# A new order of VectorE's work in the attention groups: key counts in two halves around the masks, zero ranks ahead of the queries

## What is computed

```python
h = _layernorm(x) * (1 + ca) + sa
q, k, v = (sparsify(proj(w), keep=1) for w in (wq, wk, wv))   # the largest |feature| of 16 is kept
scores = q @ k.T / sqrt(16), causal
keep the 64 largest scores of each row, softmax over them, times v, times wo
x = x + ga * attention
h = _layernorm(x) * (1 + cb) + sb
x = x + gb * experts(h)      # each expert takes its 512 best tokens of 4096
```

## Time and profile before

| | |
|---|---|
| median of 3 runs | 1072.18 us (1070.66 to 1073.46) |
| the profiled execution's own time | 1072.58 us |
| its span, first to last instruction | 1070.7 us |
| TensorE (PE) busy | 919.0 us, 86% |
| VectorE (DVE) busy | 662.1 us, 62% |
| ScalarE (ACT) busy | 480.0 us, 45% |
| GpSimd (POOL) busy | 270.0 us, 25% |
| mean granted TensorE clock | 0.912 |

### The profile page before, as it was taken

How to read it: one execution, slowest core, us unless ns; L and a number is a source line. 1 busy time by engine, 2 the same in 40 slices (tenths; PEclk the granted TensorE clock), 3 DMA queues, 4 the chain that set the end, 5 groups by cost and what they waited for, 6 DMA issues and landing times. The chain is left out here.

```text
span 1070.7 us, 17237 instructions
## 1 busy us (share of the span) xinstructions
PE 919.0 (86%) x6504; PEld 497.5 (46%) x6504; DVE 662.1 (62%) x1462; ACT 480.0 (45%) x631; POOL 270.0 (25%) x403
## 2 busy tenths in 40 slices
PE   6778999898999888999999999996213999999996
PEld 4533443334444453534335445335102666666664
DVE  6758667567677666686784784625486655543441
ACT  2635667764667746476665554661000122221110
POOL 3503212411322402132320210001003433334222
PEclk9779999999999989999988998897555999999999
DMA  4000000000100001100002012001651144442211
GB/s 149 10 1 21 1 21 1 2 1 2 60 21 1 1 27 56 60 1 2 2 1 81 2 41 81 1 1 40 219 197 41 46 114 105 113 114 40 25 20 20
DMA packets 34854, 46.57 MB, mean 43 GB/s; under 512 B 2184, under 2 KB 30928, under 8 KB 34640
## 3 DMA queue, kind: packets, MB, share of 16 engines
q1 hardware_dynamic: 28624, 36.89, 10.3%
q0 software_dynamic: 6144, 8.52, 4.9%
HBM read 32.69 MB, written 12.72 MB: 42 GB/s over the span
## 5 line engine op out<-in xcount | busy, mean ns | idle before, releaser
L947 ACT ACTIVATE p_buf<-ps 128x1024 f32<-128x1024 f32 x288 | 279.4, 1023 | 182.7 <-PE ps L424 98.7
L424 PE MATMUL ps<-qx,kd 32*128 32x512 f32 (+3 forms) x1280 | 149.0, 542 | 29.9 <-DVE p_buf L1281 26.1
L457 PE MATMUL ps<-p_buf,vv 128*17 128x512 f32 (+3 forms) x1664 | 160.2, 487 | 0.0
L2096 ACT ACTIVATE h_t<-ps,b_t 128x512 f32<-128x512 f32 x64 | 44.0, 687 | 239.7 <-PE ps L2036 239.7
L1281 DVE SCALAR_TENSOR_TENSOR p_buf<-ps,p_buf 128x1024 f32<-128x1024 f32 x64 | 76.7, 1220 | 76.6 <-ACT p_buf L947 63.5
L2036 PE MATMUL ps<-tok_t,w_sb 128*128 128x512 f32 x256 | 114.2, 605 | 0.5 <-DVEq L2143 0.5
L2046 PE MATMUL ps<-w_sb,h_t 128*128 128x256 f32 x512 | 112.5, 380 | 0.8 <-ACT h_t L2096 0.8
L779 POOL TENSOR_SCALAR_AFFINE_SELECT p_buf<-p_buf 128x512 f32<-128x512 f32 x64 | 42.0, 669 | 274.2 <-ACT p_buf L947 271.5
L2046 PEld LDWEIGHTS ps<-w_sb,h_t 128*128 128x128 f32 x512 | 96.6, 190 | 15.3 <-ACT h_t L2096 1.6
L424 PEld LDWEIGHTS ps<-qx,kd 32*128 32x128 f32 x1280 | 55.8, 193 | 72.5 <-issue 57.1
L365 PE MATMUL ps<-w_t,h_t 128*128 128x512 f32 (+1 forms) x224 | 78.8, 496 | 0.8 <-ACT w_t L889 0.8
(11 more groups left out here) (293 smaller groups left out, 1392.9 us busy)
## 6 DMA issues: line engine op xcount, KB each, us to landing
w_sb<-in_L_ffn_w_dram SPq DMA_DIRECT2D x16, 1024.0 KB, 8.5
h_table<-xr SPq DMA_DIRECT2D x3, 1056.0 KB, 4.6
x_in<-in_L_attn_x_dram SPq DMA_DIRECT2D x6, 512.0 KB, 3.9
out_dram<-xr SPq DMA_DIRECT2D x3, 1024.0 KB, 5.2
xr<-in_L_attn_x_dram SPq DMA_DIRECT2D x3, 1024.0 KB, 5.7
h_table<-xr SPq DMA_DIRECT2D x2, 528.0 KB, 3.1
xr<-in_L_attn_x_dram SPq DMA_DIRECT2D x2, 512.0 KB, 5.4
p_buf<-in_L_wmod_dram SPq DMA_DIRECT2D x1, 1024.0 KB, 8.6
```

The lines of the kernel that those rows point to most:

```text
L424: m = pe.matmul(o, key, qx[r, par, t0:t0 + w], start=True, stop=not early)
L457: m = pe.matmul(ps[32 * h:32 * h + HD + 1, 6, o:o + w], vv[:, (gi // NG) % 2, i, HG * (gi % NG) + h, :], p_of(gi, u)[:, h, lo:lo + w], sta ...
L947: act.activation(p_of(gi, u)[:, 2 * a:2 * a + 2, :], buf(w), ACT.Exp, scale=0.25).then_inc(free_of(w)[0], 1)
L2096: act.activation(h1_t[:, f, :], ps[:, L1_BANKS[f % 3], :], ACT.Relu, bias=b1_t[:, e * FO + f:e * FO + f + 1]).then_inc(s_h1, 1)
```

## The change

It touches VectorE's queue alone; no instruction of another engine moves. `key_counts` becomes `counts_first` (tokens 0 to 511, waits for K0 only) ahead of the second masks and `counts_second` (tokens 512 to 1023, waits for K1, starts from the copied last count) behind them. `keys` becomes `key_maxima`, `key_kinds` and `keys_shifted`; the turned outputs are written between them. `zero_rank` moves ahead of `queries`. The `one_feature` step of the second tile moves behind the second masks, that of the third behind the shifted keys, that of the fourth behind `losers`; `feature_limits` also goes behind `losers`. `normalize(b + 1, 0)` moves from ahead of the second masks to behind the turned outputs.

```diff
-                def key_counts(n):
-                    kx = kd[:, n % 2, :]
+                def counts_first(n):
+                    h = slice(0, 512)
+                    dve.wait_ge(f_mfree, m_at["K0", n] + 1)
+                    dve.tensor_scalar(k_not[:, h], kd[:, n % 2, h], 0.0, None, ALU.is_le)
+                    dve.drain()
+                    dve.tensor_tensor_scan(left[:, h], k_not[:, h], minus1[:, :].to_broadcast([P, 512]), TOPK + 0.5,
+                                           ALU.add, ALU.add)
+
+                def counts_second(n):
+                    h = slice(512, T)
                     dve.wait_ge(f_mfree, m_at["K1", n] + 1)
-                    dve.tensor_scalar(k_not[:, :], kx, 0.0, None, ALU.is_le)
-                    dve.drain()
-                    dve.tensor_tensor_scan(left[:, :], k_not[:, :], minus1[:, :].to_broadcast([P, T]), TOPK + 0.5,
+                    dve.drain()
+                    dve.tensor_copy(carry[:, :], left[:, 511:512])
+                    dve.tensor_scalar(k_not[:, h], kd[:, n % 2, h], 0.0, None, ALU.is_le)
+                    dve.drain()
+                    dve.tensor_tensor_scan(left[:, h], k_not[:, h], minus1[:, :].to_broadcast([P, 512]), carry[:, :],
                                            ALU.add, ALU.add)
                     dve.drain().then_inc(f_cnr, 1)
...
                     if more:
-                        key_counts(n)
-                    if g == 0 and pre:
-                        normalize(b + 1, 0)
+                        counts_first(n)
+                    mask(gi, 1, 0)
+                    mask(gi, 1, 1)
                     if tiles:
                         one_feature(b + 1, t0 + 1)
-                    mask(gi, 1, 0)
-                    mask(gi, 1, 1)
+                    if more:
+                        counts_second(n)
                     if post and g == norm_group(b - 1):
                         second_norm(b - 1, 1)
                     if g == 1 and pre:
                         norm_stats(b + 1, 1)
                     if more:
-                        keys(n)
-                    if tiles:
-                        one_feature(b + 1, t0 + 2)
+                        key_maxima(n)
+                    if more and not (post and g == norm_group(b - 1)):
+                        key_kinds(n)
                     out_rows_of(gi, 0)
+                    if g == 0 and pre:
+                        normalize(b + 1, 0)
+                    if more and post and g == norm_group(b - 1):
+                        key_kinds(n)
...
                     if more:
-                        queries(n)
+                        keys_shifted(n)
+                    if tiles:
+                        one_feature(b + 1, t0 + 2)
                     if g == 0 and post:
                         residual(b - 1, 0)
                     if more:
                         zero_rank(n)
+                    if more:
+                        queries(n)
                     if g == 1 and pre:
                         normalize(b + 1, 1)
                     if g == 0 and pre:
                         modulate(b + 1, 0)
+                    if more:
+                        losers(n)
                     if tiles:
                         one_feature(b + 1, t0 + 3)
                     if g == 3 and pre:
                         feature_limits(b + 1)
-                    if more:
-                        losers(n)
                     if g == 0 and post:
                         residual(b - 1, 1)
```

More of the change, by code:

```diff
@@ L1217, in feature_limits, with key_maxima @@
                     dve.drain()
-                def key_counts(n):
-                    kx = kd[:, n % 2, :]
+                def counts_first(n):
[7 more added lines that the diff above has]
+                    h = slice(512, T)
                     dve.wait_ge(f_mfree, m_at["K1", n] + 1)
-                    dve.tensor_scalar(k_not[:, :], kx, 0.0, None, ALU.is_le)
                     dve.drain()
-                    dve.tensor_tensor_scan(left[:, :], k_not[:, :], minus1[:, :].to_broadcast([P, T]), TOPK + 0.5,
+                    dve.tensor_copy(carry[:, :], left[:, 511:512])
+                    dve.tensor_scalar(k_not[:, h], kd[:, n % 2, h], 0.0, None, ALU.is_le)
+                    dve.drain()
+                    dve.tensor_tensor_scan(left[:, h], k_not[:, h], minus1[:, :].to_broadcast([P, 512]), carry[:, :],
                                            ALU.add, ALU.add)
                     dve.drain().then_inc(f_cnr, 1)
-                def keys(n):
-                    par = n % 2
-                    kx = kd[:, par, :]
+                def key_maxima(n):
+                    kx = kd[:, n % 2, :]
                     dve.tensor_tensor_scan(mx[:, :], kx[:, 0:512], kx[:, 0:512], 0.0, ALU.max, ALU.max)
@@ L1236, in keys, with key_kinds @@
                     dve.scalar_tensor_tensor(kb[:, :], k_not[:, 0:P], FAR, kx[:, 0:P], ALU.mult, ALU.add)
-                    dve.scalar_tensor_tensor(k_one[:, :, :], kx[:, 0:P].unsqueeze(1).to_broadcast([P, HG, P]), 0.0,
+                def key_kinds(n):
+                    par = n % 2
+                    dve.scalar_tensor_tensor(k_one[:, :, :], kd[:, par, 0:P].unsqueeze(1).to_broadcast([P, HG, P]), 0.0,
                                              onesz[:, :, :], ALU.is_gt, ALU.mult)
@@ L1242, in keys, with keys_shifted @@
                     dve.tensor_tensor(k_max[:, :], mx[:, 511:512], k_max1[:, :], ALU.max)
+                def keys_shifted(n):
+                    par = n % 2
+                    kx = kd[:, par, :]
                     dve.drain()
```

## The result

The changed kernel takes 1084.83 us (median of 4 runs, 1081.95 to 1089.48), the kernel before took 1071.42 us in the same session: a ratio of 1.0129, 95% interval 1.0102 to 1.0156, so 13.4 us slower. The forecast was 4.2 us slower: right in sign, and out by 9 us in size.

A forecast was written before the change was run, and what follows sets the result against it. TensorE sets the pace up to the second masks, VectorE from there to the losers (the tail). Profiled 1072.58 + 0.8 (groups) + 3.4 (clock) = 1076.8 us, 1076.4 against the median; range 1066 to 1085.

The forecast's parts named there:

- the clock: TensorE's clock falls behind new stalls where TensorE sets the pace: plus 3.4 us for two falls.
- `pv(gi, 8)` waits for GpSimd: In groups 3, 7, 11 `pv(gi, 8)` stalls 1.3 to 1.4 us, as GpSimd's `tri(gi, 8)` comes later.
- tails and masks without it: The sum's other terms over all groups: earlier second masks against longer VectorE work from there to the losers; -3.1 us.
- these seven: New TensorE stalls: ends of groups 0 (about 3 us), 1, 5, 9 (about 2), `pv(gi, 8)` in 3, 7, 11 (1.4).
- the price of 1.7 us: Cost of one clock fall in TensorE's time where TensorE sets the pace: 0.43 x 4 = 1.7 us.
- rival 4: The clock falls at most of the new stalls: 5 more x 1.7 = 8.5 us, 1085 us; chance 0.05.
- No stall at `lost` in g = 1: Sign of being wrong: in groups 1, 5, 9 TensorE was expected to wait about 2 us there or at the turned input.
- the 0.7 taken between bounds of 0 and 1.4: Extra us for `counts_second` directly behind a one-feature step, where GpSimd's `keep` runs beside it.
- Rival 3: `keep` and `counts_second` fully exclude each other, and a late `keep` delays the next eviction: 1080 to 1084 us; chance 0.13.
- under 6: Sign of being right: TensorE's stalls on the second masks fall from 26.1 us to under 6.
- Rival 1: Faster: the masks' stall is the bound and tails have room, 1060 us; weaker form 1068 to 1069; together chance 0.24.
- rival 5: Masks still late since exps of unit 4 come later, so tails grow without a gain: 1090 us; chance 0.02.

The follow-up runs named there:

- experiment 4: The changed kernel plus zero-weight matmuls for TensorE in its longest stalls: 1077.81 us, ratio 1.0041 to the kernel before.
- experiment 10: The changed kernel plus zero-weight matmuls in TensorE's longest stalls and GpSimd's `tri(gi, 8)` ahead of `stage(gi + 2)` in groups 2, 6, 10: 1075.13 us, ratio 1.002.
- experiment 8: The changed kernel with `counts_second` ahead of the second tile's one-feature step instead of behind it: 1084.37 us, ratio 1.012.
- experiment 7: The changed kernel with `queries` ahead of `zero_rank` again: 1098.02 us, ratio 1.021.
- experiment 9: The changed kernel with GpSimd's `tri(gi, 8)` ahead of `stage(gi + 2)` in groups 2, 6, 10: 1082.60 us, ratio 1.0101.
- Experiments 1 and 2: First, the kernel before with only `key_counts` split: 1095.74 us, ratio 1.0213; second, the changed kernel with the split undone: 1064.85 us, ratio 0.9935.
- experiment 5: The kernel before with the split alone, plus nine zero-weight matmuls ahead of `zero_rank` in eight groups: 1084.90 us, ratio 1.0105.

## Why the forecast was right in sign and short in size

The forecast's total was its sum, 0.8 us, and 3.4 us for the clock. Told apart by the ratios of the experiments (1% is 10.7 us, each good to some 2 to 3 us), the 13.8 us of 1.0129 fall into three parts:

| | forecast | measured | from |
|---|---|---|---|
| the clock (what the added matmuls take off) | 3.4 | 9.4 | 1.0129 less 1.0041 |
| `pv(gi, 8)` waits for GpSimd | 3.9 | 2.3 to 3.0 | 1.0041 less 1.002; 1.0129 less 1.0101 |
| tails and masks without it | -3.1 | 2.1 | 1.002 |

(The forecast's 3.9 is the three stalls of 1.3 in its groups 2, 6, 10, and -3.1 the rest of its 0.8. The 9.4 is a gain measured on the changed kernel alone; as said at experiment 4, the kernel before might gain by such matmuls too, and the last row would then be larger by as much.)

So two terms failed, the clock by 6.0 us and the tails by 5.2, while `pv(gi, 8)` was put 0.9 to 1.6 too high.

**The clock is the first step that failed.** "If two of these seven bring a fall, plus 3.4" was too small twice over. Of the seven stalls three brought a fall (groups 0, 1 and 5 of the profiled run), but falls also came behind stalls that the forecast didn't list, those ahead of the logits in 7, 11 and 13. The kernel before had a lowered clock over these logits as well (0.77, 0.90 and 0.68 while they ran); after the change it was 0.50, 0.50 and 0.68, so it is groups 7 and 11 in which the longer stall made it worse. And the price of 1.7 us, taken from short falls, doesn't fit where a fall lies over the logits: those run alone at the end of a group, and in group 7 they took 2.3 us longer than before, the `lost` and the first scores behind them still at 0.50. The rule the forecast gave for it holds: falls in the tails cost little (before, groups 1 and 9 with one took 44.0 us and group 5 without one 43.8), falls behind the new stalls a lot (groups 1, 5, 7 and 11 become 1.0 to 2.8 us shorter each when the matmuls are added). The attention of the changed kernel has as much of the upper clock as before, and pays more for the rest. My rival 4 (most of the listed stalls bring a fall, 1085, at a chance of 0.05) was near in kind, but its time is luck: only three of the seven did, and the tails, which it took from my sum, were 5 us longer.

**The list of stalls was right in place for some, wrong for others.** Group 0's came at `lost`, 4.04 us for about 3. In groups 1, 5 and 9 I put about 2 us at `lost` or the turned input; it was 3.2 to 3.4 us at `zero_rank`, since the late count and the turned outputs stand ahead of it there, and at `lost` little was left (0.60 us in group 9, less in 1 and 5). "No stall at `lost` in g = 1" was one of my signs of being wrong, and it came true. In 7, 11 and 13 the wait stood ahead of the logits, 2.8 to 2.9 us, where the kernel before had 1.16 us in group 7 and 0.2 in 11 and 13: group 3, which I read for all of them, has no logits.

**The tails are the second step that failed:** 2.1 us measured for a forecast of -3.1. With the two other costs taken out (experiment 10) the groups differ from before by +2.4, +2.9, +2.4 in 1, 5, 9 (forecast +2.0 each), -0.3, +1.3, +0.1 in 2, 6, 10 (forecast without the stall -0.6, +0.9, -0.6), -0.3, +0.5, +0.8 in 3, 7, 11 (-0.4 each), -3.3 and -3.0 in 4 and 8 (-3.0 each), -1.2 in 12 (-1.3), +1.3 in 13 (+0.6), -2.1 in 14 (-0.9). Of these all are within 1.2 us, and all but groups 4, 8 and 14 lie 0.1 to 1.2 above: no single place, a little in most tails. Two terms are part of it:

- `counts_second` behind a one-feature step took 1.2 us more than without it, for the 0.7 taken between bounds of 0 and 1.4; the 0.5 more, in six groups, is 3.0 us if all of it reaches the end. The comparison went from 0.42 to 1.36 us beside a `keep` of 1.16. The Trainium skill (SBUF — State Buffer, SBUF: two separate sides) describes such a wait for the whole of the other instruction, for a VectorE instruction with two SBUF inputs, as the forecast said, and also for one in a 2-port mode. The comparison has one input, so only the second case could cover it, and no view shows its mode. Rival 3's time was near as well (1080 to 1084). What the collision costs the kernel is not shown: experiment 8 removes it, but brings ScalarE's wait for the late `keep` in its place, and the time is the same.
- The queries, behind `zero_rank` now, run into `tri(gi, 8)`. Not foreseen. Group 7 before, then after:

```profile
386.00 1.22 DVE L1251 SCALAR_TENSOR_TENSOR uq<-qx,left 128x1024 bf16<-128x1024 f32 x1
389.81 1.23 POOL L779 TENSOR_SCALAR_AFFINE_SELECT p_buf<-p_buf 128x512 f32<-128x512 f32 x2 [14.48 <-ACT p_buf L947]
```

```profile
400.24 2.49 POOL L779 TENSOR_SCALAR_AFFINE_SELECT p_buf<-p_buf 128x512 f32<-128x512 f32 x2 [13.60 <-ACT p_buf L947]
400.58 1.65 DVE L1268 SCALAR_TENSOR_TENSOR uq<-qx,left 128x1024 bf16<-128x1024 f32 x1
402.16 0.65 DVE L1269 TENSOR_SCALAR q_has<-qx 128x128 bf16<-128x128 f32 x1
402.93 1.13 DVE L1284 SCALAR_TENSOR_TENSOR lw<-ps,y_mx,tie 128x128 bf16<-128x128 f32 x4
```

GpSimd's two instructions take 2.49 for 1.23 us, and the three of the queries 2.9 for 2.1, right ahead of the losers. No run separates what this costs the kernel, because moving the queries away costs more and makes them meet `keep` instead (experiment 7).

In group 0 the profile after shows +4.3, of which 3.4 are the chance named above, so 0.9 for a forecast of 0 (0.7 in experiment 9).

**What held.** The masks' wait fell to 7.0 us, nearly the "under 6" of the forecast. VectorE idles 3.75 us ahead of the masks in group 1 ("some 3"). `pv` of unit 8 waited in groups 3, 7, 11, 1.03 us each (1.3 to 1.4):

```profile
373.93 1.06 PE L457 MATMUL ps<-p_buf,vv 128*17 128x384 f32 x16 [1.03 <-POOL p_buf L779]
```

Groups 4 and 8 are 3.3 and 2.7 us shorter (3.0). And outside groups 4, 8, 12 and 14 the tail, not the masks, sets a group's end: the split alone shortens the masks' wait and costs 22 us, and without the split the masks wait longer and the kernel is faster. Rival 1 fell with them, and so did rival 5.

**What stays open.** Experiments 1 and 2 show that the split costs about 2% with or without the moves. Experiments 4 and 5 show that about half as much comes off when the clock is kept up; how much of that the kernel before would gain in the same way wasn't tried. The other half, 11 us in experiment 5, I put down to fifteen counts of some 2 us less what the earlier masks return, which no run shows; which groups pay it in full wasn't tried one by one, and neither was the collision of the queries by itself.

## What to carry to other kernels

When two engines take turns, work moved from before a hand-over to behind it can cost its full length there, however long the wait it shortens: read the tail to the next hand-over first, and make the move only in groups in which that tail is covered. Then ask what TensorE does right behind each new wait: if its work there sets the pace, the lower clock can cost as much again as the wait (2.86 and 2.8 us in group 7), and matmuls with zero weights in the wait show how much the clock costs there, if the kernel before is run with them too. Read one group of each kind, also of kinds that differ only by a step at the end.

## What the runs showed of the hardware

- Matmuls whose weights are zero kept the granted clock up through a stall: 1.00 for 0.54 in 311 to 315 us, and 9 us for the whole kernel. Adding 87 matmuls to a queue that was waiting made the kernel faster.
- The mean granted clock says little of what it costs: 0.95 in the attention of the faster kernel, 0.96 in that of the slower one.
- GpSimd can lose more than VectorE where the two meet: two of its instructions went from 1.23 to 2.49 us beside one of VectorE's that went from 1.22 to 1.65.
